# A macaron block on one NeuronCore: second batch's quantisation behind the first batch's parts, one unit's keys on ScalarE's queue, three small operations of each stage on GpSimd

## The chip, the cores and the metric

The kernel runs on one core of a Trainium2 chip. The metric is device microseconds of one execution. A NeuronCore has a matrix engine (TensorE, PE in the rows; its weight loads are PEld), VectorE (DVE), ScalarE (ACT), GpSimd (POOL) and SyncE (SP), each with an instruction stream of its own that runs in order; they wait for one another through semaphores. SP and ScalarE also issue the DMA transfers of this kernel; a DMA instruction on an engine's queue waits its turn behind what stands ahead of it on that engine.

## What is computed

The input is `x`, 8 batches of 512 rows of 128 features. The reference applies three residual steps to it:

```python
def reference(x, ...):
    x = x + 0.5 * ffn(layernorm(x), weight, bias, delta_w, delta_act)      # "f1"
    x = x + attention(layernorm(x), wq, bq, wk, bk, wv, bv)                # "pj" and what follows
    x = x + 0.5 * ffn(layernorm(x), weight, bias, delta_w, delta_act)      # "f2"
    return x

def attention(x, ...):            # 16 heads of 8 features
    xq, xk, xv = (x @ w.T + b).reshape(bs, seq_len, H, HD) for q, k, v
    xq, xk = rope(xq), rope(xk)
    scores = einsum('bhqd,bhkd->bhqk', q, k) / sqrt(HD)
    return einsum('bhqk,bhkd->bhqd', softmax(scores), v)

def ffn(x, ...):                  # blockwise fake quantisation to 4 bits, then a product
    x_q = mxfp4_pseudo_quant(x, delta_act)         # blocks of 32 features
    w_q = mxfp4_pseudo_quant(weight, delta_w)
    return einsum('bsd,od->bso', x_q, w_q) + bias

def mxfp4_pseudo_quant(x, delta):
    amax = max(abs(block)); e = floor(log2(max(amax, TINY)))
    scale = where(amax > 0, exp2(e - 2), 1) * exp2(0.5 * tanh(4 * delta))
    xs = block / scale
    q = sign(xs) * fp4_round(clip(abs(xs), 0, 6))
    return scale * q
```

## The kernel before, in words

All of `x` lies in SBUF (`xres`), a batch as 4 tiles of 128 rows. The kernel runs `slot(b)` for b from -2 to 8, and each slot has 32 steps. Every engine has its own copy of this loop. In step s of slot b the attention of batch b handles one (head, key half) pair: two transposed score products into `st` (`scoresT`), two exponentials on ScalarE (`exp`, `probs`), and every other step the product with the values (`times_v`, into `ot`). Fifteen steps ahead of that, TensorE computes the same scores untransposed into `sc` (`scores`), VectorE takes their row maxima (`maxima`, `negmax`, two per step, 16 per unit of four heads), GpSimd splits a unit's 16 maxima into three bf16 parts (`split_max`), TensorE turns them (`turn_max`), and they are loaded as extra rows of the query features. TensorE takes its instructions in the order written: a transposition that waits holds up the scores behind it.

Queries and keys are kept as three bf16 parts whose sum is the f32 value. After the projection (`project`, `copy_qk`) they get their rope (`rotate`: a product, a product with the pairs swapped by DMA (`swap_pairs`), a sum; for q and then for k), and the parts: `high` (ScalarE), `rest` (f32 less high), `mid` (ScalarE), `low`. Six DMAs on SP write them to DRAM (`write_parts`); when all six have landed (`parts_out`), `load_features` on SP reads them back in the layout of the score products, 24 rows of 2048 bf16 per DMA, three for q and three for k of each unit of four heads. Of the first batch, ScalarE's queue loads the keys of the first two units (`load_keys`). Scores of a unit wait for all six of its loads.

Each of the three norm stages of a batch (`f1`, `pj`, `f2`) runs as `stats` and `aggregate` on VectorE (`mv`), then two 128x4 operations: `ve` (variance plus epsilon) and `nm` (minus the mean); then `rstd` and `nb` on GpSimd (a power, 1 us, and a product) and the normalisation `xn`. A feed-forward stage goes on with the block scales (`block_scales`, rows 0 to 4 of the tile `amax`: largest value, exponent, scale, inverse, and inverse times a factor `invf`), the scaled product (`scale`, `xs`), three operations on VectorE (`exponents`: `xc`, `p`, `magic`), and three more (`quant`: `xs`, `p`, `xq`), then TensorE turns `xq`, ScalarE copies it (`copy_xqT`), TensorE multiplies (`mul_w`) and VectorE adds (`add_ffn`). The rows write `p` for the tile `p2` and `_f` for `_f1` and `_f2`.

Tables of steps set the order (`FFN1`, `PROJ`, `FFN2`): an operation with step t is issued in step t mod 32, in the slot that t div 32 says. `FIRST` overrides them for some stages of the first batches. Batch 0's projection, batch 0's and 1's first feed-forward and the last batch's second are `hurried`: VectorE does more of their work, and without spreading it between maxima. Two lines of the tables matter here:

```python
FIRST["f1", 1] = dict(stats=-16, rstd=-15, norm=-10, amax=-8, scale=-7, expo=-3, quant=-2, turn=8, mul=9)
FIRST["pj", 1] = dict(PROJ, stats=11, rstd=12, norm=14)
```

`("f1", 1)` is the first feed-forward of the second batch. Its `scale` and `quant` run on GpSimd (`hurried_rows` is false for it), its `exponents` on VectorE.

Of the kernel before, what the change touches and what calls it, by code (L numbers as in the profile page):

```python
# [78 lines left out]
FIRST["f1", 1] = dict(stats=-16, rstd=-15, norm=-10, amax=-8, scale=-7, expo=-3, quant=-2, turn=8, mul=9)  # L79
FIRST["pj", 1] = dict(PROJ, stats=11, rstd=12, norm=14)  # L80
# [4 lines left out]
def macaron_kernel(nc, x, wq, bq, wk, bk, wv, bv, w, bias, delta_w, delta_act, ident_in, rope_in, out):  # L85
# [5 lines left out]
    with ExitStack() as ctx:  # L91
# [142 lines left out]
        def hurried_rows(n, b):  # L234

            return hurried(n, b) and (n, b) != ("f1", 1)

# [60 lines left out]
        def _(sp):  # L298
# [38 lines left out]
            def load_features(b, par, half):  # L337
# [8 lines left out]
                for g in (2 * half, 2 * half + 1):  # L346
# [31 lines left out]
        def _(pool):  # L378
# [40 lines left out]
            def rstd(n, b):  # L419

                k, s = bufs[n], LN[n]
                pool.wait_ge(s["stats"], 3 * b + 3)
                if after(b):
                    pool.wait_ge(s["norm"], b)
                nc.gpsimd.tensor_tensor(k["rstd"][:, :], k["ve"][:, :], nhalf[:, :], ALU.pow).then_inc(s["rstd"], 1)  # L425
                pool.wait_ge(s["rstd"], 2 * b + 1)
# [82 lines left out]
            def slot(b, par):  # L509
                for s in range(STEPS):  # L510
# [32 lines left out]
        def _(act):  # L543
# [29 lines left out]
            def norm(n, b, half):  # L573

                k, s = bufs[n], LN[n]
                if half == 0:
                    act.wait_ge(s["rstd"], 2 * b + 2)
# [65 lines left out]
            def load_keys():  # L643
# [3 lines left out]
                for g in range(2):  # L647
                    heads = slice(UH * g, UH * (g + 1))
                    k = scratch_k[0, :, :, heads, :].rearrange("d a h s -> (d a) (h s)")
                    for c in range(PARTS):  # L650
                        act.dma_start(feat["k"][0][PARTS * HD * c:PARTS * HD * (c + 1), heads, :]
                                      .rearrange("r h s -> r (h s)"), k).then_inc(feat_loaded[g], 16)
# [18 lines left out]
            def slot(b, par):  # L671
                for s in range(STEPS):
# [14 lines left out]
                    if b == -2 and s == FIRST["f1", 0]["rstd"]:  # L687
# [31 lines left out]
        def _(dve):  # L719
# [52 lines left out]
            def stats(n, b):  # L772
# [8 lines left out]
                if after(2 * b):  # L781
                    dve.wait_ge(s["rstd"], 2 * b)
# [4 lines left out]
            def aggregate(n, b):  # L787

                k, s = bufs[n], LN[n]
                dve.wait_ge(s["stats"], 3 * b + 1)  # L790
# [152 lines left out]
            def slot(b, par):  # L943
                for s in range(STEPS):
# [23 lines left out]
                    for n, first in (("f2", -1), ("f1", 2)):  # L968
                        for nb, _ in turns(b, par, s, n, "amax", first):
                            block_scales(n, nb, 0)  # L970
                            if hurried(n, nb):
                                for step in range(1, 5):
                                    block_scales(n, nb, step)
                        for later in (1, 2):
                            for nb, _ in turns(b, par, s, n, "amax", first, later=later):
                                if not hurried(n, nb):
                                    block_scales(n, nb, 2 * later)
# [237 lines left out]
```

## Time and profile before

| | us |
|---|---|
| median of 3 runs | 534.62 |
| lowest, highest | 534.57, 535.41 |
| the profiled execution | 534.99 |
| its span, first to last instruction | 533.2 |

| engine | busy us | share of the span |
|---|---|---|
| TensorE | 455.7 | 85% |
| VectorE | 437.7 | 82% |
| ScalarE | 383.2 | 72% |
| GpSimd | 234.0 | 44% |

Times in the rows below are microseconds from the start of the span. In a timeline row the first number is the start, the second the time from the start to the end of the group, then engine, line, operation, output and inputs, shapes and count; in brackets stands how long the engine had been idle before it and what ended that. An engine's share of busy time is an average over a start in which little overlaps (up to some 53 us), a steady part and an end with one batch alone.

### The profile page before, as it was taken

The numbers are of one execution on the slowest core, as the hardware profiler recorded it, in microseconds if no ns is written. First come the engines' busy times: TensorE is split into PE (matmuls) and PEld (weight loads), VectorE is DVE, ScalarE is ACT, GpSimd is POOL, SyncE is SP. The second block draws the span as 40 slices with busy tenths as digits, with TensorE's granted clock in tenths as the row PEclk, the third lists the DMA queues.
The fourth block names the chain that finished last, engine by engine and source line by source line (L and its number), as shares of the span: only waits on it lengthen the run. The fifth ranks groups of instructions, "written<-read, shape, count | busy, mean of one in ns | idle before, by whom it ended". The sixth has DMA issues, their size and how long they took to land.

```text
span 533.2 us, 8358 instructions
## 1 busy us (share of the span) xinstructions
PE 455.7 (85%) x2564; PEld 153.0 (29%) x2564; DVE 437.7 (82%) x996; ACT 383.2 (72%) x750; POOL 234.0 (44%) x340
## 2 busy tenths in 40 slices
PE   2252999999989998999999998999899989998941
PEld 1121232333223232333233323323232323222211
DVE  6863999898899889997999799988997889897125
ACT  7854158678778887787868887787787877777730
POOL 8330065336644465545553656356543624112200
PEclk9985599999999999999999999999999999999995
DMA  5015311321122213221222112221222132100000
GB/s 163 23 49 139 89 52 51 90 92 50 51 90 91 68 36 94 73 75 33 78 77 87 59 51 90 91 71 50 91 85 67 30 91 91 50 2 2 22 0 20
DMA packets 27960, 34.86 MB, mean 65 GB/s; under 512 B 6278, under 2 KB 21260, under 8 KB 27916
## 3 DMA queue, kind: packets, MB, share of 16 engines
q1 hardware_dynamic: 26068, 33.35, 20.6%
q10 hardware_dynamic: 1848, 0.98, 0.7%
q8 instruction: 20, 0.33, 0.3%
q14 instruction: 24, 0.20, 0.1%
HBM read 21.34 MB, written 8.39 MB: 56 GB/s over the span
## 4 chain that ended last, share of the span: by engine, by line
PE 57%; DVE 24%; issue 7%; ACT 5%; POOL 4%; DMA 2%; SPq 0%; POOLq 0%; ACTq 0%; DVEq 0%
PE ot L1138 17%; PE sc L1125 16%; DVE negmax L915 13%; PE st L1114 12%; ACT probs L668 3%; PE misc L1063 2%; PE misc L1080 2%; PE misc L1103 2%; DVE stats_f L784 1%; PE misc L1088 1%; PE misc L1096 1%; PE misc L1058 1%; DMA feat_q<-parts_q 1%; PE misc L1071 1%; PE misc L1047 1%
## 5 line engine op out<-in xcount | busy, mean ns | idle before, releaser
L915 DVE TENSOR_REDUCE negmax<-sc 128x1 f32<-128x512 f32 x512 | 329.6, 682 | 49.2 <-PE sc L1125 48.9
L668 ACT ACTIVATE probs<-st 128x512 f32<-128x512 f32 x512 | 272.7, 599 | 76.9 <-PE st L1114 74.8
L1125 PE MATMUL sc<-feat_k,feat_q 96*128 96x512 bf16 x512 | 186.7, 393 | 18.2 <-DVE negmax L915 10.3
L1114 PE MATMUL st<-feat_q,feat_k 99*128 99x512 bf16 x512 | 155.9, 380 | 8.0 <-ACT probs L668 7.8
L1138 PE MATMUL ot<-probs,vfeat 128*32 128x512 f32 x1024 | 136.2, 604 | 1.1 <-ACT probs L668 1.0
L1125 PEld LDWEIGHTS sc<-feat_k,feat_q 96*128 96x128 bf16 x512 | 49.7, 97 | 169.0 <-DVE negmax L915 101.7
L1114 PEld LDWEIGHTS st<-feat_q,feat_k 99*128 99x128 bf16 x512 | 49.4, 98 | 78.0 <-ACT probs L668 48.9
L466 POOL TENSOR_SCALAR maxparts<-negmax 128x16 bf16<-128x16 f32 x32 | 8.5, 266 | 73.4 <-DVE negmax L915 73.4
L450 POOL TENSOR_TENSOR xs_f<-xc_f,magic_f 128x512 f32<-128x512 f32 x14 | 17.8, 1270 | 36.9 <-DVE magic_f L878 36.9
L425 POOL TENSOR_TENSOR rstd_f<-ve_f,nhalf 128x4 f32<-128x4 f32 x16 | 16.6, 1035 | 37.0 <-DVE nm_f L796 31.7
L1138 PEld LDWEIGHTS ot<-probs,vfeat 128*32 128x32 f32 x1024 | 20.2, 108 | 37.5 <-ACT probs L668 20.0
L443 POOL TENSOR_TENSOR xs_f<-xn_f,amax_f 128x512 f32<-128x512 f32 x14 | 14.7, 1047 | 31.2 <-DVE amax_f L821 31.2
L1047 PE MATMUL misc<-identb,xq_f 128*128 128x128 bf16 x64 | 6.8, 234 | 21.4 <-DVE xq_f L859 17.4
L583 ACT ACTIVATE xn_f<-xres,nb_f,rstd_f 128x128 f32<-128x128 f32 x56 | 24.4, 490 | 0.9 <-POOL nb_f L427 0.9
L506 POOL TENSOR_TENSOR xres<-xres,onorm 128x256 f32<-128x256 f32 x15 | 10.9, 726 | 27.5 <-DVE onorm L931 27.5
L592 ACT COPY xqT_f<-misc 128x512 bf16<-128x512 bf16 x16 | 9.6, 600 | 18.2 <-PE misc L1047 18.2
L485 POOL TENSOR_TENSOR qkswap<-qkswap,ropeT 128x512 f32<-128x512 f32 x14 | 17.8, 1273 | 10.4 <-DMA qkswap<-qkpre 10.4
L425 POOL TENSOR_TENSOR rstd_pj<-ve_pj,nhalf 128x4 f32<-128x4 f32 x8 | 8.3, 1034 | 31.9 <-DVE nm_pj L796 31.9
L883 DVE TENSOR_TENSOR xres<-xres,misc 128x512 f32<-128x512 f32 x16 | 10.9, 683 | 11.8 <-PE misc L1063 11.3
L922 DVE RECIPROCAL recip<-misc 128x32 f32<-128x32 f32 x16 | 5.6, 349 | 16.6 <-PE misc L1103 16.6
L547 ACT COPY feat_k<-zeroone 32x4096 f32<-32x4096 f32 (+1 forms) x4 | 14.4, 3599 | 6.3 <-issue 6.3
L452 POOL TENSOR_TENSOR p_f<-xs_f,magic_f 128x512 f32<-128x512 f32 x14 | 18.1, 1293 | 1.1
(134 smaller groups left out, 461.3 us busy)
## 6 DMA issues: line engine op xcount, KB each, us to landing
feat_q<-parts_q SPq DMA_DIRECT2D x96, 96.0 KB
feat_k<-parts_k SPq DMA_DIRECT2D x90, 96.0 KB
qkswap<-qkpre SPq DMA_DIRECT2D x32, 128.0 KB, 2.0
parts_q<-qkparts_q SPq DMA_DIRECT2D x24, 128.0 KB, 2.3
parts_k<-qkparts_k SPq DMA_DIRECT2D x24, 128.0 KB, 2.3
xres<-in_L_attn_x_dram SPq DMA_DIRECT2D x8, 256.0 KB, 4.9
out_dram<-xres SPq DMA_DIRECT2D x8, 256.0 KB, 2.5
feat_k<-parts_k ACTq DMA_DIRECT2D x6, 96.0 KB
```

What stands on the lines that cost most here:

```text
L425: nc.gpsimd.tensor_tensor(k["rstd"][:, :], k["ve"][:, :], nhalf[:, :], ALU.pow).then_inc(s["rstd"], 1)
L443: nc.gpsimd.tensor_tensor(blocks(k["xs"][:, :]), blocks(k["xn"][:, :]), per_block(k["amax"][:, 4, :]), ALU.mult).then_inc(s["scaled"], 1)
L450: nc.gpsimd.tensor_tensor(k["xs"][:, :], k["xc"][:, :], k["magic"][:, :], ALU.add).then_inc(s["quant"], 1)
L452: nc.gpsimd.tensor_tensor(k["p2"][:, :], k["xs"][:, :], k["magic"][:, :], ALU.subtract).then_inc(s["quant"], 1)
L485: nc.gpsimd.tensor_tensor(qkswap[:, i, :], qkswap[:, i, :], ropeT[:, 1, :], ALU.mult).then_inc(rope_step, 1)
L547: nc.scalar.copy(feat[n][i][low:low + count, :, :].rearrange("r h s -> r (h s)").bitcast(F32), zeroone[low:low + count, value:value + 1].b ...
L583: ins = nc.scalar.activation(k["xn"][:, t * D:(t + 1) * D], xb(b, t * D, D), ACT.Identity, bias=k["nb"][:, t:t + 1], scale=k["rstd"][:, t: ...
L668: nc.scalar.activation(probs[:, s % US, j * S:(j + 1) * S], st[:, bank(2 * s + j), :], ACT.Exp, scale=SCALE).then_inc(exp_done, 1)
L915: nc.vector.tensor_reduce(negmax[:, g, j:j + 1], sc[:, bank(16 * g + j), :], AX.X, ALU.max, negate=True).then_inc(sc_maxed, 1)
L1114: nc.tensor.matmul(st[:, bank(2 * s + j), :], feat["k"][par][0:MROWS, h, kb * P:(kb + 1) * P], feat["q"][par][0:MROWS, h, :], start=True, ...
L1125: nc.tensor.matmul(sc[:, bank(16 * g + j), :], feat["q"][par][0:SROWS, h, t * P:(t + 1) * P], feat["k"][par][0:SROWS, h, :], start=True, s ...
L1138: ins = nc.tensor.matmul(ot[VW * i:VW * (i + 1), :], vfeat[par][:, kb, UH * g + i, :], probs[:, UH * (kb // 2) + i, S * (kb % 2):S * (kb % ...
```

## The change

Four edits.

1. The second batch's first feed-forward: `expo` and `quant` move from steps -3 and -2 to step 9 (of slot -1), `turn` and `mul` two steps later, and its `quant` runs on VectorE. `scale` stays on GpSimd. The statistics of its projection move two steps later.
2. ScalarE's `load_keys` loads the keys of the first unit only, and stands ahead of the second batch's `copy_xqT`. SP loads the second unit's keys, between that unit's queries.
3. `ve` and `nm` of every norm stage run on GpSimd, in front of `rstd`.
4. The last row of the block scales (inverse times `invf`) runs in front of `scale`, on `scale`'s engine: GpSimd for all stages but the first batch's first and the last batch's second feed-forward.

```diff
-FIRST["f1", 1] = dict(stats=-16, rstd=-15, norm=-10, amax=-8, scale=-7, expo=-3, quant=-2, turn=8, mul=9)
-FIRST["pj", 1] = dict(PROJ, stats=11, rstd=12, norm=14)
+FIRST["f1", 1] = dict(stats=-16, rstd=-15, norm=-10, amax=-8, scale=-7, expo=9, quant=9, turn=10, mul=11)
+FIRST["pj", 1] = dict(PROJ, stats=13, rstd=14, norm=16)
...
@@ SP, load_features
-                        if (b, half) != (0, 0):
+                        if (b, g) != (0, 0):
...
@@ GpSimd, rstd
-                pool.wait_ge(s["stats"], 3 * b + 3)
+                pool.wait_ge(s["stats"], 2 * b + 2)
                 if after(b):
                     pool.wait_ge(s["norm"], b)
+                nc.gpsimd.tensor_scalar(k["ve"][:, :], k["mv"][:, :, 1], EPS, None, ALU.add).then_inc(s["rstd"], 1)
+                nc.gpsimd.tensor_scalar(k["nm"][:, :], k["mv"][:, :, 0], -1.0, None, ALU.mult).then_inc(s["rstd"], 1)
+                pool.wait_ge(s["rstd"], 4 * b + 2)
                 nc.gpsimd.tensor_tensor(k["rstd"][:, :], k["ve"][:, :], nhalf[:, :], ALU.pow).then_inc(s["rstd"], 1)
...
@@ GpSimd, scale (the same two lines on VectorE)
+                pool.wait_ge(s["scale"], 5 * b + 4)
+                nc.gpsimd.tensor_scalar(k["amax"][:, 4, :], k["amax"][:, 2, :], invf[:, 0:1], None, ALU.mult).then_inc(s["scale"], 1)
...
@@ GpSimd, slot
-                            if not hurried_rows(n, nb):
+                            if not hurried(n, nb) or (n, nb) == ("f1", 1):
                                 scale(n, nb)
                         for nb, _ in turns(b, par, s, n, "quant", first):
-                            if not hurried_rows(n, nb):
+                            if not hurried(n, nb):
                                 quant(n, nb)
...
@@ ScalarE, load_keys and slot
-                for g in range(2):
-                    heads = slice(UH * g, UH * (g + 1))
+                heads = slice(0, UH)
...
+                    if b == -1 and s == FIRST["f1", 1]["turn"]:
+                        load_keys()
                     if b == -1 and s == PROJ["load"][0] % STEPS:
-                        load_keys()
                         feature_rows("k", 1, 1)
...
@@ VectorE, aggregate
-                dve.wait_ge(s["stats"], 3 * b + 2)
-                nc.vector.tensor_scalar(k["ve"][:, :], k["mv"][:, :, 1], EPS, None, ALU.add)
-                nc.vector.tensor_scalar(k["nm"][:, :], k["mv"][:, :, 0], -1.0, None, ALU.mult).then_inc(s["stats"], 1)
```

The order of the instructions shows three places. On VectorE in the start, from the first rope product of batch 0 (`qkT`, `qkswap`) to its `low` (`qkparts` from `qkrest`), before:

```order
L890 TENSOR_TENSOR qkT_q<-qkpre,ropeT 128x512
L870 TENSOR_SCALAR xc_f<-xs_f 128x512
L874 TENSOR_SCALAR p_f<-xc_f 128x512
L878 TENSOR_SCALAR magic_f<-p_f 128x512
L893 TENSOR_TENSOR qkswap<-qkswap,ropeT 128x512
L895 TENSOR_TENSOR qkT_q<-qkT_q,qkswap 128x512
L890 TENSOR_TENSOR qkT_k<-qkpre,ropeT 128x512
L893 TENSOR_TENSOR qkswap<-qkswap,ropeT 128x512
L895 TENSOR_TENSOR qkT_k<-qkT_k,qkswap 128x512
L901 TENSOR_TENSOR qkrest_q<-qkT_q,qkparts_q 128x512
```

and the end of the same stretch now, from the last two operations of the parts to the first maxima:

```order
L898 TENSOR_TENSOR qkrest_k<-qkT_k,qkparts_k 128x512
L904 TENSOR_TENSOR qkparts_k<-qkrest_k,qkparts_k 128x512
L867 TENSOR_SCALAR xc_f<-xs_f 128x512
L871 TENSOR_SCALAR p_f<-xc_f 128x512
L875 TENSOR_SCALAR magic_f<-p_f 128x512
L850 TENSOR_TENSOR xs_f<-xc_f,magic_f 128x512
L852 TENSOR_TENSOR p_f<-xs_f,magic_f 128x512
L856 TENSOR_TENSOR xq_f<-p_f,amax_f 128x512
L880 TENSOR_TENSOR xres<-xres,misc 128x512
L785 BN_STATS stats_pj<-xres 128x6 x4
L793 BN_AGGR mv_pj<-stats_pj 128x2 x4
L912 TENSOR_REDUCE negmax<-sc 128x1 x37
```

The three `exponents` left the place behind the first rope product and stand, with the three operations of `quant` that were GpSimd's, behind the last `low`, ahead of the add, the statistics and the first maxima. On ScalarE, at the same time, from the last part to the fill of feature rows, before:

```order
L627 CAST qkparts_k<-qkrest_k 128x512
L592 COPY xqT_f<-misc 128x512
L651 DMA feat_k<-parts_k 24x2048 x6
L547 COPY feat_k<-zeroone 3x4096
L583 ACTIVATE xn_pj<-xres,nb_pj,rstd_pj 128x128 x4
```

and now:

```order
L628 CAST qkparts_k<-qkrest_k 128x512
L651 DMA feat_k<-parts_k 24x2048 x3
L593 COPY xqT_f<-misc 128x512
L548 COPY feat_k<-zeroone 3x4096
L584 ACTIVATE xn_pj<-xres,nb_pj,rstd_pj 128x128 x4
```

The key loads went from six to three and in front of the copy of the second batch's `xq`. On GpSimd in a steady batch, from the split of a unit's maxima (`maxparts`, `maxrest`) to the quantisation of the first feed-forward, now:

```order
L467 TENSOR_SCALAR maxparts<-negmax 128x16
L469 TENSOR_TENSOR maxrest<-negmax,maxparts 128x16
L471 TENSOR_SCALAR maxparts<-maxrest 128x16
L473 TENSOR_TENSOR maxparts<-maxrest,maxparts 128x16
L421 TENSOR_SCALAR ve_f<-mv_f 128x4
L422 TENSOR_SCALAR nm_f<-mv_f 128x4
L424 TENSOR_TENSOR rstd_f<-ve_f,nhalf 128x4
L426 TENSOR_TENSOR nb_f<-nm_f,rstd_f 128x4
L438 TENSOR_SCALAR amax_f<-amax_f,invf 128x16
L444 TENSOR_TENSOR xs_f<-xn_f,amax_f 128x512
```

Before, `ve`, `nm` and the `amax` row stood on VectorE, between maxima; the other seven rows stood here in this order.

## Rows read from the trace of the kernel before

**Rows 1.** Busy time by stretch: TensorE, weight loads, VectorE, ScalarE, GpSimd, clock, DMA.

```profile
46.00:52.60 6.60, 0.00 (x0) 0.00 (x1) 1.19 (x9) 3.50 (x1) 1.22 (x2) 0.50 0.61 158
...
60.00:67.50 7.50, 7.42 (x17) 2.80 (x18) 6.59 (x11) 0.84 (x2) 0.94 (x4) 0.50 0.02 4
...
193.20:250.09 56.89, 54.20 (x321) 18.30 (x320) 51.36 (x119) 45.12 (x93) 30.37 (x42) 1.00 0.23 71
```

**Rows 2.** Chain that ended last, in order of time (start, length), around the loads.

```profile
43.56 2.30 DMA parts_k<-qkparts_k
...
47.58 4.98 DMA feat_q<-parts_q
```

**Rows 3.** Timeline of VectorE in the start (start, length).

```profile
33.45 1.20 DVE L893 TENSOR_TENSOR qkswap<-qkswap,ropeT 128x512 f32<-128x512 f32 x1 [0.69 <-DMA qkswap<-qkpre]
...
37.70 0.68 DVE L893 TENSOR_TENSOR qkswap<-qkswap,ropeT 128x512 f32<-128x512 f32 x1
...
39.02 0.68 DVE L901 TENSOR_TENSOR qkrest_q<-qkT_q,qkparts_q 128x512 f32<-128x512 f32 x1
...
42.37 0.69 DVE L907 TENSOR_TENSOR qkparts_k<-qkrest_k,qkparts_k 128x512 bf16<-128x512 f32 x1 [0.68 <-ACT qkparts_k L627]
44.98 0.69 DVE L883 TENSOR_TENSOR xres<-xres,misc 128x512 f32<-128x512 f32 x1 [1.92 <-PE misc L1063]
...
46.60 0.38 DVE L792 BATCH_NORM_AGGREGATE mv_pj<-stats_pj 128x2 f32<-128x6 f32 x4
...
53.24 10.86 DVE L915 TENSOR_REDUCE negmax<-sc 128x1 f32<-128x512 f32 x18 [5.99 <-PE sc L1125]
```

**Rows 4.** Timelines of GpSimd and ScalarE in the start.

```profile
35.85 1.38 POOL L456 TENSOR_TENSOR xq_f<-p_f,amax_f 128x512 bf16<-128x512 f32 x1
...
32.51 3.60 ACT L547 COPY feat_k<-zeroone 32x4096 f32<-32x4096 f32 x1
36.35 0.62 ACT L623 CAST qkparts_q<-qkT_q 128x512 bf16<-128x512 f32 x1 [0.25 <-DVE qkT_q L895]
...
45.93 3.12 ACTq L651 DMA_DIRECT2D feat_k<-parts_k  x6
```

**Rows 5.** Timeline of VectorE at the end: quantisation to residual add.

```profile
522.80 0.43 DVE L870 TENSOR_SCALAR xc_f<-xs_f 128x512 f32<-128x512 f32 x1
...
529.77 0.69 DVE L883 TENSOR_TENSOR xres<-xres,misc 128x512 f32<-128x512 f32 x1 [3.44 <-PE misc L1063]
```

**Rows 6.** Timelines of VectorE, TensorE and GpSimd in a steady batch.

```profile
198.59 0.37 DVE L792 BATCH_NORM_AGGREGATE mv_f<-stats_f 128x2 f32<-128x6 f32 x4
...
199.19 3.07 DVE L915 TENSOR_REDUCE negmax<-sc 128x1 f32<-128x512 f32 x5
...
204.66 0.42 DVE L870 TENSOR_SCALAR xc_f<-xs_f 128x512 f32<-128x512 f32 x1
...
199.93 0.39 PE L1125 MATMUL sc<-feat_k,feat_q 96*128 96x512 bf16 x1 [0.47 <-DVE negmax L915]
...
199.96 0.25 POOL L466 TENSOR_SCALAR maxparts<-negmax 128x16 bf16<-128x16 f32 x1 [0.78 <-DVE negmax L915]
...
202.38 1.05 POOL L443 TENSOR_TENSOR xs_f<-xn_f,amax_f 128x512 f32<-128x512 f32 x1
```

**Rows 7.** Groups of small operations by shape: count, busy us, mean ns.

```profile
L466 POOL TENSOR_SCALAR maxparts<-negmax 128x16 bf16<-128x16 f32 x32 | 8.5, 266 | 73.4 <-DVE negmax L915 73.4
...
L427 POOL TENSOR_TENSOR nb_pj<-nm_pj,rstd_pj 128x4 f32<-128x4 f32 x8 | 1.6, 201 | 0.6
...
L412 POOL TENSOR_SCALAR biasr<-biasp,ident 3x256 f32<-3x256 bf16 x1 | 0.9, 912 | 0.1
...
L821 DVE TENSOR_SCALAR amax_f<-amax_f,invf 128x16 f32<-128x16 f32 x16 | 3.7, 234 | 0.1
```

**Rows 8.** Timelines of VectorE and GpSimd in the last norm stage.

```profile
517.15 0.38 DVE L792 BATCH_NORM_AGGREGATE mv_f<-stats_f 128x2 f32<-128x6 f32 x4
...
517.88 1.04 POOL L425 TENSOR_TENSOR rstd_f<-ve_f,nhalf 128x4 f32<-128x4 f32 x1 [20.15 <-DVE nm_f L796]
```

More of the change, by code:

```diff
@@ L232, in hurried @@
             return (n, b) in (("f1", 0), ("pj", 0), ("f1", 1), ("f2", B - 1))
-        def hurried_rows(n, b):
-            return hurried(n, b) and (n, b) != ("f1", 1)
         def qk_bank(b, j):
@@ L421, in rstd @@
                 k, s = bufs[n], LN[n]
-                pool.wait_ge(s["stats"], 3 * b + 3)
+                pool.wait_ge(s["stats"], 2 * b + 2)
                 if after(b):
                     pool.wait_ge(s["norm"], b)
+                nc.gpsimd.tensor_scalar(k["ve"][:, :], k["mv"][:, :, 1], EPS, None, ALU.add).then_inc(s["rstd"], 1)
+                nc.gpsimd.tensor_scalar(k["nm"][:, :], k["mv"][:, :, 0], -1.0, None, ALU.mult).then_inc(s["rstd"], 1)
+                pool.wait_ge(s["rstd"], 4 * b + 2)
                 nc.gpsimd.tensor_tensor(k["rstd"][:, :], k["ve"][:, :], nhalf[:, :], ALU.pow).then_inc(s["rstd"], 1)
-                pool.wait_ge(s["rstd"], 2 * b + 1)
+                pool.wait_ge(s["rstd"], 4 * b + 3)
                 nc.gpsimd.tensor_tensor(k["nb"][:, :], k["nm"][:, :], k["rstd"][:, :], ALU.mult).then_inc(s["rstd"], 1)
@@ L576, in norm @@
                 if half == 0:
-                    act.wait_ge(s["rstd"], 2 * b + 2)
+                    act.wait_ge(s["rstd"], 4 * b + 4)
                     if n == "pj" and after(b):
@@ L646, in load_keys @@
                 act.wait_ge(parts_out, 96)
-                for g in range(2):
-                    heads = slice(UH * g, UH * (g + 1))
[L649 to L652, printed above, removed]
+                heads = slice(0, UH)
+                k = scratch_k[0, :, :, heads, :].rearrange("d a h s -> (d a) (h s)")
+                for c in range(PARTS):
+                    act.dma_start(feat["k"][0][PARTS * HD * c:PARTS * HD * (c + 1), heads, :]
+                                  .rearrange("r h s -> r (h s)"), k).then_inc(feat_loaded[0], 16)
             def copy_out(b, g):
@@ L780, in stats @@
                     dve.wait_ge(x_attended, 2 * b + 2)
-                if after(2 * b):
-                    dve.wait_ge(s["rstd"], 2 * b)
+                if after(b):
+                    dve.wait_ge(s["rstd"], 4 * b)
                 for t in range(T):
@@ L789, in aggregate @@
                 k, s = bufs[n], LN[n]
-                dve.wait_ge(s["stats"], 3 * b + 1)
+                dve.wait_ge(s["stats"], 2 * b + 1)
                 for t in range(T):
@@ L815, in block_scales @@
                     nc.vector.tensor_scalar(m[:, 3, :], m[:, 1, :], TINY_FLOOR, 0.25, ALU.max, ALU.mult).then_inc(s["scale"], 1)
-                elif step == 3:
+                else:
                     dve.wait_ge(s["scale"], a + 3)
                     nc.vector.reciprocal(m[:, 2, :], m[:, 3, :]).then_inc(s["scale"], 1)
-                else:
-                    dve.wait_ge(s["scale"], a + 4)
-                    nc.vector.tensor_scalar(m[:, 4, :], m[:, 2, :], invf[:, 0:1], None, ALU.mult).then_inc(s["scale"], 1)
             def blocks(ap):
@@ L831, in norm @@
                 k, s = bufs[n], LN[n]
-                dve.wait_ge(s["rstd"], 2 * b + 2)
+                dve.wait_ge(s["rstd"], 4 * b + 4)
                 if n != "pj" and b > 0:
@@ L842, in scale @@
                 k, s = bufs[n], FF[n]
+                dve.wait_ge(s["scale"], 5 * b + 4)
+                nc.vector.tensor_scalar(k["amax"][:, 4, :], k["amax"][:, 2, :], invf[:, 0:1], None, ALU.mult).then_inc(s["scale"], 1)
                 dve.wait_ge(s["scale"], 5 * b + 5)
@@ L971, in slot @@
                             if hurried(n, nb):
-                                for step in range(1, 5):
+                                for step in range(1, 4):
                                     block_scales(n, nb, step)
[L974 to L977, printed above, removed]
+                        for nb, _ in turns(b, par, s, n, "amax", first, later=1):
+                            if not hurried(n, nb):
+                                block_scales(n, nb, 2)
                         for nb, _ in turns(b, par, s, n, "scale", first):
-                            if hurried_rows(n, nb):
+                            if hurried(n, nb) and (n, nb) != ("f1", 1):
                                 scale(n, nb)
```

2 lines of the change are left out of this document (1 added, 1 removed).

## The prediction, made before the changed kernel had run

> **What bounds the kernel now.** I first read busy time by stretch, then the chain that ended last, then the instructions of each engine in order. In the steady part one batch takes 56.89 us, with TensorE busy 54.20 and VectorE 51.36 of it [rows 1]: TensorE has some 2.7 us of gaps in a batch, and only VectorE work that causes such a gap is worth anything. Before the steady part TensorE does nothing at all between 46.0 and 52.6 us [rows 1]. So there are two stages to cost: the start (up to the first row maximum at 53.24 us [rows 3]) and the repeated batch; then the end, where the last batch runs alone.
>
> In the start the chain runs through the first batch's rope and parts. The last of six stores of the parts is issued at 43.56 and lands 2.30 us later; the loads go out, the last query load of the first unit is issued at 47.58 and lands 4.98 us later [rows 2]; then scores begin. The reader is to see in the VectorE rows that the same kind of instruction, a two-input 128x512 operation, takes 1.20 us at 33.45 but 0.68 at 37.70 [rows 3], and in the GpSimd rows that the second batch's quantisation (three such operations in a row, the last from 35.85) runs until 37.23, just before the fast one [rows 4].
>
> **The start, step by step.** *Quantisation moved behind the parts.* The three `exponents` operations stood before the rope's swap product, which waited 0.69 us longer for its DMA anyway [rows 3]: taking them out gains nothing there. What gains is that GpSimd is silent during the rope. From the swap product at 33.45 to the first `rest` at 39.02 are five operations in 5.57 us. At the undisturbed spacing of the pair 37.70 to 39.02 (two in 1.32; I take 0.71 each, since the second hand-over is shortened) they need 3.55. One loss stands ahead of it: `rstd` of the first projection norm now has the two small operations on GpSimd, +0.25 (costed under the tail). So `rest` starts at 33.45 + 0.25 + 3.55 = 37.25 instead of 39.02: **-1.77**. It needs the high part from ScalarE, which has a 3.60 us fill from 32.51 in front of it [rows 4]: fill end 36.36 with the +0.25, copy 0.62 [rows 4], so 37.0, just in time. Behind it the chain of parts and stores is unchanged, so the stores land at 45.86 - 1.77 = 44.1.
>
> *Loads.* Now ScalarE issues six key loads, 3.12 us from 45.93 [rows 4], beside SP's query loads. From 46.0 to 52.6 the DMA engines move 158 GB/s [rows 1], 1.04 MB, or 10.6 loads of 24 rows of 2048 bf16 (98 KB; the shape stands with the change), while the first unit needs six: the second unit's keys on ScalarE's queue went ahead of the first unit's queries. With three of them moved to SP, behind the first unit's queries, some two to three loads fewer stand ahead: 2.5 x 6.6/10.6 = 1.5 us. Bounds: nothing, and the four and a half loads that are too many, 2.8. I take 1.4, near the middle: scores could begin 3.2 us earlier and the first maximum stand at 50.1; with nothing, at 51.5.
> The Trainium skill, DMA: Bandwidth & Descriptors, section SWDGE vs HWDGE vs iDMA, says that a DMA engine takes its queues in turn. By that rule SP's three query loads had to let only three key loads pass, and removing the fourth to sixth would change nothing, so the first maximum would stand at 51.5 and the sum come to rival 1's; the 10.6 loads moved by the landing speak against it here.
>
> *What is late next.* VectorE. The second batch's quantisation now lies between the parts and the first maximum: the last `low` ends at 43.06 - 1.77 = 41.3 (it ran from 42.37 for 0.69 [rows 3]). The same sequence, alone, stands at the end of the program: from `xc` at 522.80 to the end of the residual add, 529.77 + 0.69, 7.66 us, TensorE's transposes and products included [rows 5]. ScalarE's copy in it now stands behind the key loads, which wait for the stores: 44.1 + three issues of 0.52 = 45.7, against 45.55 when the copy could start, +0.2. The add ends at 49.15; statistics and aggregation follow it as now, from the add's end at 45.67 to 46.98 [rows 3], 1.3 us. So VectorE is free at 50.45, later than the 50.1 of the loads, and the first maximum starts there: 53.24 - 50.45 = **-2.8**. If the loads gain nothing: -1.8. The second unit's keys, now between the queries on SP, are 12 loads in at 0.62 each from 45, some 53, and wanted 16 maxima of 0.60 after 50.4 [rows 3], at 60; that costs nothing.
>
> **The repeated batch.** *`ve` and `nm` off VectorE.* Only one of the three norm stages of a batch has TensorE waiting on VectorE, the one of the second feed-forward. There the aggregation ends at 198.96 and the next maximum starts at 199.19 [rows 6]; without the two it follows the aggregation at once, which is 0.23 less, or up to 0.08 more where neighbouring operations overlap, as the next operation here starts before the one ahead is shown as ended; I take 0.29. TensorE's next score sat idle 0.47 for a maximum there [rows 6], so the shift is passed on. In the other norm stages of the batches, twelve, VectorE waits for TensorE soon after and I cost them at nothing; uncovered, they would be worth the same again. Seven stages on the path: 7 x 0.29 = **-2.0**. Bounds: 0, if the next wait takes it up, and -5.5 with the other twelve.
>
> *`amax` times the inverse off VectorE:* it is the last small operation of its stage, behind which VectorE waits for TensorE again, so nothing; uncovered, fourteen times 0.23 [rows 7], 3.3. What GpSimd does next waited for it before too.
>
> *On GpSimd* the three operations lengthen the queue: the split of the maxima starts at 199.96, the scaled block product `xs` runs from 202.38 to 203.43, and VectorE wants that at 204.66 [rows 6]: 1.23 us in hand. Prices: a 128x16 scalar operation took 0.27, a 128x4 one 0.20; the pointer-scalar form on 3x256 took 0.91 [rows 7]. These have 4 to 16 elements per partition, so I go by the first two: 0.27 + 0.22 + 0.30 with gaps, about 0.85. 0.4 us remain in hand, so nothing is late. The split stands ahead of them in the queue and is not delayed.
>
> **The tail.** In the last feed-forward the aggregation ends at 517.53 and `rstd` starts at 517.88 [rows 8]. These 0.35 us hold VectorE's two operations and the hand-over. On GpSimd the two take 0.27 + 0.22 = 0.49; if VectorE's share of the 0.35 is between 0.1 and 0.35, the loss is 0.14 to 0.39: I take **+0.25** (by the 0.91 price, 1.5). The multiplication stays on VectorE there.
>
> **Sum.** -2.8 - 2.0 + 0.25 = -4.55. The profiled execution took 534.99 (span 533.2), 0.37 above the median of the runs; on the median of 534.62 I forecast **530.0**.
>
> **Rivals.**
> 1. *The start gains only what the rope gains* (loads not helped, or ScalarE held longer before the copy that the second batch's product, and behind it all scores, wait for): -1.8 instead of -2.8, 531.1. For it: two paths end within 0.4 us of each other. 18%.
> 2. *The steady relief is taken up* by TensorE's other gaps or by ScalarE: -2.55 in all, 532.1. For it: TensorE is at 95%. Against: its gap at this place is released by the maximum. 15%.
> 3. *VectorE's relief is worth more*: the stages costed at nothing, and the first batch, give another 1 to 2 us: 528.5. 15%.
> 4. *The clock returns earlier.* From 60.0 to 67.5 TensorE is busy 7.42 of 7.50 us at a granted 0.50, 1.2 GHz [rows 1]. If the shorter idle stretch brings 2.4 GHz sooner, at most half of the dense part from 62 on, some 2 us: 527.8. Against: the idle stretch keeps some 8 us. 6%.
> 5. *Slower.* GpSimd's three operations outlast the 1.23 us in hand, VectorE's `xc` waits and with it every maximum queued behind, in seven batches. Net zero is reached where the three take 1.88 together (7 x (1.88 - 1.52) = 2.55). At the pointer price of 0.91 each they take 2.73: +8.5 in the batches, -2.8 at the start, +1.5 in the tail, 541.8. 5%.
> 6. *No net change* (rival 1 with rival 2 and a longer tail), 534: 5%.
>
> The forecast itself has 36%. A measurement of this kernel tells changes of over 0.2%, 1.07 us. Faster 0.89, same 0.06, slower 0.05. The range takes in rivals 1 to 3 and part of 4: 527.4 to 532.6; the forecast's own is 529 to 531.
>
> **What would show it.** The rope's operations on VectorE at 0.69 with GpSimd idle; `rest` near 37.3; the first score near 49.5 and the first maximum near 50.4 right behind the aggregation; a batch period near 56.6; no wait of `xc` for `xs`; `rstd` in the last stage 0.25 later behind its aggregation. Wrong would make it: GpSimd's small operations at over 0.6 us, key loads that still land at 50.8, or a period that stays at 56.89.

## The result, and the profile after

| | before | changed |
|---|---|---|
| median, us | 534.77 | 528.59 |
| lowest, highest | 534.57, 535.41 | 528.04, 529.05 |
| span of the profiled execution | 533.2 | 527.2 |
| busy: TensorE, VectorE, GpSimd | 455.7, 437.7, 234.0 | 454.2, 429.1, 245.8 |

The ratio is 0.9886 (95% interval 0.9874 to 0.9898): 6.2 us or 1.1% faster, where 4.55 were forecast. Both medians are of four runs. A second series gave 528.51 against 534.72, ratio 0.9890 (0.9875 to 0.9905).

**The start.** VectorE, then ScalarE and TensorE, in the timeline of the changed kernel; the rows answer to [rows 3] and [rows 4].

```profile
33.26 0.69 DVE L890 TENSOR_TENSOR qkswap<-qkswap,ropeT 128x512 f32<-128x512 f32 x1 [1.95 <-DMA qkswap<-qkpre]
...
35.20 0.68 DVE L890 TENSOR_TENSOR qkswap<-qkswap,ropeT 128x512 f32<-128x512 f32 x1
...
36.52 0.68 DVE L898 TENSOR_TENSOR qkrest_q<-qkT_q,qkparts_q 128x512 f32<-128x512 f32 x1
...
39.87 0.69 DVE L904 TENSOR_TENSOR qkparts_k<-qkrest_k,qkparts_k 128x512 bf16<-128x512 f32 x1 [0.68 <-ACT qkparts_k L628]
40.48 0.42 DVE L867 TENSOR_SCALAR xc_f<-xs_f 128x512 f32<-128x512 f32 x1
...
47.87 0.69 DVE L880 TENSOR_TENSOR xres<-xres,misc 128x512 f32<-128x512 f32 x1 [3.87 <-PE misc L1059]
...
49.49 0.38 DVE L793 BATCH_NORM_AGGREGATE mv_pj<-stats_pj 128x2 f32<-128x6 f32 x4
50.04 2.48 DVE L912 TENSOR_REDUCE negmax<-sc 128x1 f32<-128x512 f32 x4 [0.17 <-PE sc L1121]
...
35.58 0.62 ACT L624 CAST qkparts_q<-qkT_q 128x512 bf16<-128x512 f32 x1
...
43.44 1.58 ACTq L651 DMA_DIRECT2D feat_k<-parts_k  x3
45.12 0.59 ACT L593 COPY xqT_f<-misc 128x512 bf16<-128x512 bf16 x1 [5.29 <-PE misc L1043]
...
49.39 1.03 PE L1121 MATMUL sc<-feat_k,feat_q 96*128 96x512 bf16 x2 [1.57 <-DMA feat_q<-parts_q]
```

Before, TensorE's first score stood here:

```profile
52.60 2.00 PE L1125 MATMUL sc<-feat_k,feat_q 96*128 96x512 bf16 x4 [7.66 <-DMA feat_q<-parts_q]
```

Both swap products now take 0.69 and 0.68. `rest` starts at 36.52 in place of 39.02 and the loads go out at 43.44 in place of 45.93: 2.50 us earlier. From the loads' issue to the first score are 5.95 us in place of 6.67, another 0.72. The first maximum moves from 53.24 to 50.04, by 3.20. VectorE is ready for it at 49.87 and then waits 0.17 for TensorE's score, so the loads and VectorE end almost together.

**The steady batch.** Timelines of VectorE and GpSimd, which answer to [rows 6].

```profile
194.83 0.37 DVE L793 BATCH_NORM_AGGREGATE mv_f<-stats_f 128x2 f32<-128x6 f32 x4
...
195.12 3.05 DVE L912 TENSOR_REDUCE negmax<-sc 128x1 f32<-128x512 f32 x5
195.86 0.25 POOL L467 TENSOR_SCALAR maxparts<-negmax 128x16 bf16<-128x16 f32 x1 [0.43 <-DVE negmax L912]
...
197.14 0.23 POOL L421 TENSOR_SCALAR ve_f<-mv_f 128x4 f32<-128x4 f32 x1
...
199.06 0.34 POOL L438 TENSOR_SCALAR amax_f<-amax_f,invf 128x16 f32<-128x16 f32 x1
...
199.48 1.05 POOL L444 TENSOR_TENSOR xs_f<-xn_f,amax_f 128x512 f32<-128x512 f32 x1
...
200.56 0.43 DVE L867 TENSOR_SCALAR xc_f<-xs_f 128x512 f32<-128x512 f32 x1
```

The next maximum starts 0.29 after the aggregation's start, 0.60 before. GpSimd's split of the maxima (`maxparts`), which waits for them, comes earlier with it: 1.03 after the aggregation's start, 1.37 before. From the split's start, `xs` ends at 4.67 in place of 3.47, so the three small operations lengthen GpSimd's row by 1.20 us. VectorE's `xc` starts 4.70 behind the split in both kernels. Of the 1.23 us in hand 0.03 are left; `xc` does not wait in a steady batch, but nothing is left in hand.

**Tail, and busy time by stretch** (columns as in [rows 1]). The tail's rows answer to [rows 8].

```profile
510.83 0.38 DVE L793 BATCH_NORM_AGGREGATE mv_f<-stats_f 128x2 f32<-128x6 f32 x4
511.30 0.23 POOL L421 TENSOR_SCALAR ve_f<-mv_f 128x4 f32<-128x4 f32 x1 [19.88 <-DVE mv_f L793]
...
511.92 1.04 POOL L424 TENSOR_TENSOR rstd_f<-ve_f,nhalf 128x4 f32<-128x4 f32 x1
```

```profile
60.00:67.50 7.50, 6.81 (x18) 2.55 (x17) 6.04 (x11) 1.53 (x3) 2.01 (x5) 0.68 0.11 39
138.28:194.83 56.55, 54.19 (x320) 18.30 (x319) 50.79 (x112) 45.09 (x94) 32.48 (x51) 1.00 0.23 71
```

From the aggregation's start to `rstd` are 1.09 us, 0.73 before: +0.36. A batch takes 56.55 in place of 56.89; TensorE's busy time in it is the same, and its gaps are shorter. Read by the attention's output rows, the shift against before is 3.20 at the first maximum, 3.43 after the first batch, grows by 0.35 in each of six batches to 5.50, by 0.82 in the last to 6.32, and the tail gives 0.36 back: 5.96, the 6.0 by which the spans differ.

### The profile page after: what moved, and what is told of

The parts are those of the page before. It is cut to its first block, busy times and chain, and to the rows that moved or that the text cites. A ratio compares the mean times of both kernels' runs of the same rounds, so it can differ in the third digit from the quotient of the medians.

```text
span 527.2 us, 8358 instructions
## 1 busy us (share of the span) xinstructions
PE 454.2 (86%) x2564; PEld 152.3 (29%) x2564; DVE 429.1 (81%) x937; ACT 383.4 (73%) x750; POOL 245.8 (47%) x399
## 4 chain that ended last, share of the span: by engine, by line
PE 58%; DVE 22%; issue 7%; POOL 5%; ACT 5%; DMA 2%; SPq 0%; POOLq 0%; ACTq 0%; DVEq 0%
PE ot L1134 18%; PE sc L1121 16%; PE st L1110 12%; DVE negmax L912 12%; ACT probs L668 3%; PE misc L1059 2%; PE misc L1076 2%; PE misc L1099 2%; DVE stats_f L785 1%; PE misc L1084 1%; PE misc L1092 1%; PE misc L1054 1%; PE misc L1067 1%; PE misc L1043 1%; DVE amax_f L805 1%
## 5 line engine op out<-in xcount | busy, mean ns | idle before, releaser
L1110 PEld LDWEIGHTS st<-feat_q,feat_k 99*128 99x128 bf16 x512 | 49.4, 98 | 78.6 <-ACT probs L668 50.2
L451 POOL TENSOR_TENSOR xs_f<-xc_f,magic_f 128x512 f32<-128x512 f32 x13 | 16.5, 1273 | 29.0 <-DVE magic_f L875 29.0
L421 POOL TENSOR_SCALAR ve_pj<-mv_pj 128x4 f32<-128x4 f32 x8 | 1.8, 228 | 40.6 <-DVE mv_pj L793 40.6
L421 POOL TENSOR_SCALAR ve_f<-mv_f 128x4 f32<-128x4 f32 x16 | 3.7, 229 | 34.5 <-DVE mv_f L793 29.8
L453 POOL TENSOR_TENSOR p_f<-xs_f,magic_f 128x512 f32<-128x512 f32 x13 | 16.5, 1272 | 1.0
L785 DVE BATCH_NORM_STATS2 stats_f<-xres 128x6 f32<-128x128 f32 x64 | 13.8, 278 | 2.7 <-DMA xres<-in_L_attn_x_dram 2.6
```

The costliest lines, as they stand in the source:

```text
L451: nc.gpsimd.tensor_tensor(k["xs"][:, :], k["xc"][:, :], k["magic"][:, :], ALU.add).then_inc(s["quant"], 1)
L453: nc.gpsimd.tensor_tensor(k["p2"][:, :], k["xs"][:, :], k["magic"][:, :], ALU.subtract).then_inc(s["quant"], 1)
L785: ins = nc.vector.bn_stats(k["stats"][:, t, :], xb(b, t * D, D))
L1110: nc.tensor.matmul(st[:, bank(2 * s + j), :], feat["k"][par][0:MROWS, h, kb * P:(kb + 1) * P], feat["q"][par][0:MROWS, h, :], start=True, ...
```

## The experiments

Times are medians of 4 to 12 runs. A difference in brackets is taken from the median of before in the same series: 534.63 for experiments 1 to 3, 534.55 for 4 to 7, 534.72 for 8. 528.51 is the changed kernel's median of experiment 8; what is set against it comes from another series, so some 0.2 us of such a difference can be the series.

**1. The start alone, and the small operations alone.** Two kernels that share the change between them. `e1_start_only` is the kernel before with edits 1 and 2, `e2_small_only` the one with edits 3 and 4:

```diff
 e1: FIRST["f1", 1], FIRST["pj", 1], load_keys, load_features and quant's engine as changed
 e2: aggregate, rstd, block_scales and scale as changed
```

> The kernel before with the first two parts of the change alone: exponents and quantisation of f1 1 behind the four parts of pj 0 and on VectorE, ScalarE's queue with three key loads. ve, nm and the fourth row of amax stay on VectorE. Theory (two independent parts): the start gives about 3.0 us (first maximum at about 50.2), each batch takes 56.9 as before, the tail does not change, so the time is about 531.8. Rival (the start gets its gain from the small operations): about 534 to 534.5, and the first maximum stays near 53.

> The kernel before with the third part alone: ve, nm and the fourth row of amax on GpSimd. Theory: the start gains 0.2 us, the batches 0.35 each (2.1 to 2.5 over six to seven of them), the last batch's f2 stage about 0.8, and the tail loses 0.36, so about 531.5 to 532, with e1 the two differences add up to that of the whole change, 6.2 us, to within 0.5. Rival (the relief of a batch comes from a TensorE that is granted its clock earlier because of the earlier start): about 534.6, batches of 56.9.

Measured: 531.39 (-3.24) and 532.61 (-2.02). Batches take 56.90 in the first (4 batches, 137.71 to 365.31 by the aggregations) and 56.55 in the second (141.59 to 367.79): the relief of a batch is the small operations', the gain of the start the reordering's, and neither rival stands. The second time lies 0.6 above what was expected. The two do not add up to 6.2 to within 0.5; they fall 0.9 short. The intervals of the two ratios (0.9924 to 0.9951, 0.9941 to 0.9973) are together wider than that. In the rows, e2's first maximum is at 53.61, 0.37 later than before: its loads took 7.21 us to the first score against 6.67.

**2. The order undone.** `e3_no_reorder` is the changed kernel without edit 1; ScalarE still has three key loads, at the old place.

```diff
-FIRST["f1", 1] = dict(..., expo=9, quant=9, turn=10, mul=11)
+FIRST["f1", 1] = dict(..., expo=-3, quant=-2, turn=8, mul=9)      # and quant on GpSimd
```

> The changed kernel with its first part undone: exponents of f1 1 ahead of the parts of pj 0 and the quantisation on GpSimd again; ScalarE's queue still has three key loads, at their old place, and the small operations stay on GpSimd. Theory: the whole of the rope's 2.5 us comes from the order, and the loads get 0.2 to 0.7 for having one half less on one queue, so the time is 1.8 to 2.5 above the changed kernel, about 530.5 to 531.1. Rival (three key loads in place of six on ScalarE's queue are what the start gains): at most 0.5 above the changed kernel, about 529.

Measured: 530.87, 2.36 above the changed kernel's 528.51. The rope is back to its old pace (`rest` at 38.85), and what edit 1 gives, with the place of `load_keys` ahead of the copy, is 2.1 (first maxima) to 2.4 (medians).

It gives a second comparison: e3 differs from e2 only in the key loads. First the rows of e2, then of e3: ScalarE's loads, TensorE's first score.

```profile
45.75 3.11 ACTq L652 DMA_DIRECT2D feat_k<-parts_k  x6
...
52.96 1.46 PE L1121 MATMUL sc<-feat_k,feat_q 96*128 96x512 bf16 x3 [8.21 <-DMA feat_q<-parts_q]
```

```profile
45.78 1.57 ACTq L651 DMA_DIRECT2D feat_k<-parts_k  x3
...
51.53 2.00 PE L1120 MATMUL sc<-feat_k,feat_q 96*128 96x512 bf16 x4 [6.76 <-DMA feat_q<-parts_q]
```

7.21 us from issue to score with six, 5.75 with three. Here, where VectorE is free early, the whole difference reaches the first maximum: 53.61 to 52.17.

**3. The loads undone.** `e4_six_key_loads` is the changed kernel without edit 2's count.

```diff
-                heads = slice(0, UH)
+                for g in range(2):
+                    heads = slice(UH * g, UH * (g + 1))
```

> The changed kernel with the second part undone: six key loads on ScalarE's queue, none of the first batch's first half on SP's, still ahead of the copy of the quantised rows of f1 1. Theory: the copy starts 4.7 us later than it does with three issues of 1.58 us, so f1 1's sums come behind the first maximum, and the loads land 0.7 later: 0.7 to 2.0 above the changed kernel, about 529.3 to 530.6. Rival (the engines take their queues in turn and the number on a queue does not matter; the copy has time in hand): 0 to 0.2, about 528.7, with the first maximum at 50.0.

Measured: 529.78, 1.27 above 528.51. The copy of `xq` starts at 46.74 in place of 45.12, VectorE is free at 51.41, and the first maximum starts there, 1.37 later. The loads take 7.16, 1.2 more than in the first profile of the changed kernel, where 0.7 was expected. Theory right, on both of its paths: the loads alone would have moved the first maximum by almost as much. (The copy's delay is 1.6, three issues more, not the 4.7 that the expectation named by a slip.)

**4. GpSimd beside the rope.** `e5_gpsimd_beside_rope` adds three additions on GpSimd whose result nobody uses.

```diff
+                pool.wait_ge(qk_swapped[0], 32)
+                for i in range(3):
+                    nc.gpsimd.tensor_tensor(bufs["f2"]["p2"][:, :], xb(2), xb(2), ALU.add).then_inc(spare, 1)
+                    pool.wait_ge(spare, i + 1)
```

> The changed kernel with work added whose result nobody uses: three additions of 128x512 on GpSimd, begun when q's swapped halves have landed, so that they run beside the five operations of the rope on VectorE. Theory (the rope gained 0.74 us more than forecast because GpSimd's quantisation no longer shares the memory port with VectorE's operations of two inputs): the five operations go from 0.69 us to 0.9 to 1.2 each, the stores and loads behind them come 1 to 2.5 later, and so does the end: 529.6 to 531.1. Rival (only the exponents taken out of VectorE's queue matter): operations stay at 0.69, time within 0.2 of the changed kernel.

Measured: 530.95, 2.4 above 528.51. Timeline of VectorE and GpSimd:

```profile
33.37 4.37 POOL L466 TENSOR_TENSOR p_f<-xres 128x512 f32<-128x512 f32 x3 [4.56 <-DMA qkswap<-qkpre]
33.99 1.41 DVE L903 TENSOR_TENSOR qkT_q<-qkT_q,qkswap 128x512 f32<-128x512 f32 x1
35.33 1.52 DVE L898 TENSOR_TENSOR qkT_k<-qkpre,ropeT 128x512 f32<-128x512 f32 x1
...
36.77 1.52 DVE L901 TENSOR_TENSOR qkswap<-qkswap,ropeT 128x512 f32<-128x512 f32 x1
...
38.94 0.68 DVE L909 TENSOR_TENSOR qkrest_q<-qkT_q,qkparts_q 128x512 f32<-128x512 f32 x1
```

With the exponents still out of VectorE's queue, three operations on GpSimd give back the whole gain: `rest` at 38.94, as before the change. Three of VectorE's operations take 1.41 to 1.52 in place of 0.69, each about as long as one of GpSimd's (4.37 / 3 = 1.46). The rival is dead: what edit 1 gives is GpSimd's silence. The Trainium skill, SBUF — State Buffer, section Who interferes with whom, says that a VectorE instruction with two inputs in SBUF contends with a GpSimd instruction that reads SBUF, and that the lock on the ports they share is exclusive; the 1.46 and 1.52 agree.

**5. Two stages back on VectorE.** `e6_first_last_vectore` has `ve` and `nm` on VectorE for the first projection norm and the last feed-forward norm, and on GpSimd elsewhere.

```diff
+            return (n, b) in (("pj", 0), ("f2", B - 1))      # alone(n, b): ve and nm on VectorE
```

> The changed kernel with ve and nm on VectorE again in two stages only, pj 0 and f2 of the last batch, where GpSimd's three operations stand in a row that all else waits for. Theory: rstd of pj 0 starts 0.3 to 0.4 earlier and the rope with it, and the tail gains 0.36: 0.6 to 0.8 below the changed kernel, about 527.9. Rival (the start is bound by the swap's landing and not by rstd): only the tail's 0.36, about 528.2.

Measured: 528.13 (527.96 to 528.54), ratio to before 0.9881 (0.9869 to 0.9894). The swap product starts at 32.76 in place of 33.26, the first maximum at 49.40 in place of 50.04, and from the last aggregation to `rstd` are 0.82 in place of 1.09. The rows show both gains. The median is the lowest of the study, 6.4 below before in its own series where the changed kernel is 6.2 below, but that is less than such a measurement can tell from no change.

**6. The `amax` row.** `e7_amax_vectore` has it on VectorE again.

```diff
-                nc.gpsimd.tensor_scalar(k["amax"][:, 4, :], k["amax"][:, 2, :], invf[:, 0:1], None, ALU.mult)
+                    nc.vector.tensor_scalar(m[:, 4, :], m[:, 2, :], invf[:, 0:1], None, ALU.mult)
```

> The changed kernel with the fourth row of amax on VectorE again, ve and nm stay on GpSimd. Theory: the row is off the chain of a steady batch, so its move gives 0 per batch; in the last batch it gives the 0.5 us that the last stage gained beyond the steady relief: 0 to 0.5 above the changed kernel, 528.6 to 529.1. Rival (a third of the relief of 0.35 per batch is the row's): 0.12 x 7 = 0.8 above, about 529.4, with batches of 56.67.

Measured: 529.45, 0.9 above 528.51. The time is the rival's, the rows are not: batches take 56.55 (138.21 to 364.43, four). All of it comes at the end, 0.26 in the batch before the last and 0.53 in the last. The rows of the last batch's last unit, first e7, then the changed kernel:

```profile
483.97 0.22 DVE L817 TENSOR_SCALAR amax_f<-amax_f,invf 128x16 f32<-128x16 f32 x1
...
485.29 0.54 POOL L465 TENSOR_SCALAR maxparts<-negmax 128x16 bf16<-128x16 f32 x1
...
487.17 0.24 PE L1092 MATMUL misc<-identb,maxparts 128*48 128x128 bf16 x1 [0.97 <-POOL maxparts L471]
```

```profile
483.41 0.34 POOL L438 TENSOR_SCALAR amax_f<-amax_f,invf 128x16 f32<-128x16 f32 x1 [7.63 <-DVE amax_f L816]
...
484.84 0.25 POOL L467 TENSOR_SCALAR maxparts<-negmax 128x16 bf16<-128x16 f32 x1
...
486.42 0.24 PE L1092 MATMUL misc<-identb,maxparts 128*48 128x128 bf16 x1 [0.44 <-POOL maxparts L473]
```

On VectorE the row stands between the last maxima, and GpSimd's split of these maxima, behind `xs` in its row, starts later. Of the 0.53, 0.13 is the last maximum and 0.11 the way from it to the split. The other 0.30 is the split itself, which takes 1.88 us to TensorE's turn in e7 and before, and 1.58 in the changed kernel. But e1, with the `amax` row on VectorE, has 1.58 too, and its last batch is 0.29 shorter than before's: this part is not shown to be the row's, and why the split's operations take longer in two kernels stays open. In the batch before the last the parts do not add up: e7 loses 0.26 there, the kernel with `ve` and `nm` undone (e9) 0.37, and before, without either edit, 0.35.

**7. What GpSimd has in hand.** `e8_gpsimd_slack` adds a power, whose result nobody uses, behind `nb` of every second feed-forward but the last.

```diff
+                    nc.gpsimd.tensor_tensor(idle[:, :], k["ve"][:, :], nhalf[:, :], ALU.pow).then_inc(spare, 1)
```

> The changed kernel with work added whose result nobody uses: one more power of 1.04 us on GpSimd behind nb in the f2 stage of every batch but the last. Theory (GpSimd had 1.23 us in hand before xc, and the small operations used 0.85 of it): xs comes about 0.65 later than xc can, and every batch takes 0.65 longer: about 4.5 us above the changed kernel, 533.1. Rival (xs was never near the chain, since the maximum that it needs comes later than GpSimd's three operations): 0 to 0.3, about 528.7.

Measured: 535.33, 6.8 above 528.51 and 0.3% slower than before (ratio 1.003, 1.0017 to 1.0043). Timelines of VectorE and GpSimd:

```profile
201.48 1.05 POOL L450 TENSOR_TENSOR xs_f<-xn_f,amax_f 128x512 f32<-128x512 f32 x1
...
202.56 0.43 DVE L873 TENSOR_SCALAR xc_f<-xs_f 128x512 f32<-128x512 f32 x1 [0.88 <-POOL xs_f L450]
```

A batch takes 57.51, 0.96 more than 56.55, for an operation of 1.01: nothing was in hand, where the theory had 0.4. Seven of the twelve runs took 534.9 to 535.4 us and five 537.3 to 537.5; the profile is one of the first group, and what the others lost is not known. In one batch of the profile (310.88 to 369.85, 58.97 us) the granted clock also fell to half, from about 324.5 to 327.9, which no other kernel here showed: 1.5 us more.

**8. `ve` and `nm` on VectorE everywhere, and the changed kernel again.** `e9_stats_vectore` undoes edit 3 alone; `a1_changed_again` is the changed kernel.

```diff
+            return True      # alone(n, b)
```

> The changed kernel with ve and nm on VectorE again in every stage; only the fourth row of amax stays on GpSimd. Theory (the relief of a batch is that ve and nm no longer stand in front of a maximum on VectorE, 0.35 per batch; the amax row gives only the 0.5 of the last stage): batches of 56.9, start 0.5 earlier as in the kernel with two stages changed back, tail 0.36 earlier, less 0.3 in the last f2 stage: 7 x 0.35 + 0.3 - 0.86 = 1.9 above the changed kernel, about 530.5. Rival (the relief is GpSimd's later xs, that is the order of GpSimd's operations and not VectorE's row): batches stay at 56.55, and the time is 0.5 below the changed kernel, about 528.1.

> The changed kernel itself, beside e9 on one chip, to hold the sum of e1 and e2 against it. Both theories: 528.0 to 529.1. If the first scores start 0.3 us sooner or later than 49.39 here, with the same issue of the loads, the loading time spreads from run to run, and the 0.72 us that the loads seemed to give in the first profile is one draw of it; a fixed price would give 49.3 to 49.5.

Measured: 531.63 (-3.1) and 528.51 (-6.2). Batches of e9 take 56.88 (138.55 to 366.06, four): all but 0.02 of the relief of 0.35 is VectorE's row, and not GpSimd's. The kernel is 3.1 above the changed one, where 1.9 was expected. Of the 3.0 by which the spans differ, 0.65 is the final store: the span ends 3.37 us behind the last addition, against 2.72; and the start did not gain 0.5, it lost 0.3. The reason stands in the set-up of the first microseconds, VectorE and GpSimd, first e9, then the changed kernel:

```profile
7.11 0.53 POOL L406 TENSOR_SCALAR biasin<-biasin 3x128 f32<-3x128 f32 x1
...
8.21 0.78 DVE L759 TENSOR_TENSOR wtmp<-wtmp 128x128 f32<-128x128 f32 x1
...
10.91 0.69 DVE L814 TENSOR_REDUCE amax_f<-xn_f 128x16 f32<-128x512 f32 x1
```

```profile
7.71 0.55 POOL L402 TENSOR_SCALAR biasin<-biasin 3x128 f32<-3x128 f32 x1
...
7.90 0.29 DVE L754 TENSOR_TENSOR wtmp<-wtmp 128x128 f32<-128x128 f32 x1
...
9.83 0.69 DVE L805 TENSOR_REDUCE amax_f<-xn_f 128x16 f32<-128x512 f32 x1
```

With `ve` and `nm` of the first norm ahead of it, GpSimd's preparation of the bias starts 0.6 later, and VectorE's weight preparation passes it: VectorE is 1.08 us ahead at `amax`. That the bias work is what slows the weight preparation (0.78 against 0.29 for one product) is read from these rows alone. Part of it is given back to the same bias work, and 0.7 is left at the first projection's statistics (21.32 against 22.02). Moving the bias work out of the way altogether was not tried.

In a1 the first score comes at 49.21, 5.69 us after the loads' issue, against 49.39 and 5.95 in the first profile: between the two cases expected. Over all twelve profiles, three key loads took 5.05 to 5.95 (nine kernels, mean 5.68), six 6.67 to 7.21 (three, mean 7.01): 1.33 apart, with single profiles up to 0.63 from their mean.

## Why the prediction was right, and where its terms were off

The forecast was 530.0, measured 528.59: inside the range of 527.4 to 532.6 but below the forecast's own 529 to 531. Sign and mechanism were right and the gain too small, by 1.4 us of the span's 5.96. Term by term, in the profiled execution:

| step of the prediction | forecast | measured |
|---|---|---|
| `rest` starts | 37.25 (-1.77) | 36.52 (-2.50) |
| loads, with three keys less on ScalarE | -1.4 | -0.72 (this pair), -1.33 (means), -1.44 (e2 to e3) |
| VectorE free, first maximum | 50.45, -2.8 | 49.87, 50.04, -3.20 |
| first batch | 0 | -0.23, not traced |
| second feed-forward norm, seven stages | 7 x -0.29 = -2.0 | 6 x -0.35 - 0.28 = -2.4 |
| `amax` row | 0 | 0 in a steady batch, -0.53 in the last, 0.3 of it not shown to be the row's |
| three small operations on GpSimd | 0.85 of 1.23 in hand | 1.20 of 1.23 |
| tail | +0.25 | +0.36 |

**Rope: the right mechanism, mis-sized by 0.73.** The five operations took 3.26 and not 3.55: all have the spacing of an undisturbed pair, 0.65, where I took 0.71. The swap product came at 33.26 and not at 33.70: the small operations ahead of `rstd` cost 0.5 there and not 0.25, but GpSimd's later set-up gave 0.7, which the prediction did not look for. Experiment 4 shows that GpSimd's silence is the cause, experiment 5 the 0.5, and experiment 8 the 0.7.

**Loads: right on the mean, and by luck in the profile.** The 1.4 from "10.6 loads moved by the landing" is what e2 and e3 differ by, and near the difference of the means. My reading of the rule weighed against it (the Trainium skill, DMA: Bandwidth & Descriptors, section SWDGE vs HWDGE vs iDMA), that the fourth to sixth key load would change nothing, is not borne out: they cost 1.3 to 1.4. How they cost it, by standing ahead of the queries or by a share of the transfer engines, no run separates. In the profiled pair the loads gave only 0.72. That the path through them ended at 50.04, where 50.1 was forecast, is luck: the rope gave 0.73 more and the loads 0.68 less. "VectorE is late next" was right to within 0.2 us, since VectorE is ready 0.17 sooner; which of the two ends last changes with the loads' spread (VectorE in e1, e4, e7 and e9, the loads in the first profile). Rival 1, the loads not helping, is refuted.

**Batches: right, 0.06 small.** 0.35 is beyond the 0.29 that I took from the rows, 0.23 to 0.31; rival 2, that the relief is taken up, did not happen in any batch.

**GpSimd in hand: right by 0.03, the price too low by 0.35.** "0.4 us remain in hand, so nothing is late" came true only just. The three operations were costed at 0.85 and lengthen GpSimd's row by 1.20, of which 0.75 is `ve` and `nm` and 0.44 the `amax` row (e7 and e9, which take one of the two off GpSimd, keep 0.48 and 0.79 in hand). The 0.85 was added up from durations with small gaps. From start to start an operation takes 0.31 (`ve`, `nm`) and 0.42 (`amax`) in the changed kernel's rows, and there are hand-overs beside. Measured from the aggregation, `xs` comes only 0.86 later, which looks like the 0.85; but that is 1.20 less the 0.34 by which the split starts earlier, and `xc` comes earlier by the same 0.34. The same prices were too low in the tail (+0.36 for +0.25) and ahead of the first projection's `rstd` (0.5 for 0.25). Rival 5's point of no change, three operations of 1.88 together, does not suffer from this; the change came within 0.03 of where each further microsecond costs one, and e8 shows that side, 0.96 a batch.

**The `amax` row: missed.** It is free in a steady batch, where VectorE waits for TensorE behind it, and its move goes with 0.53 in the last batch, where the split of the last maxima stands behind `xs` on GpSimd and nothing covers it. The prediction looked at a steady batch only.

The difference of 1.4 lies in the start (0.4), the first batch (0.2), the batches (0.4) and the last batch (0.5), less 0.1 in the tail. The time came out at rival 3's 528.5, but only the first batch's part is its mechanism.

## What to carry to other kernels

Price a small operation on another engine's queue by the step from its start to the next one's start, hand-over included, and not by its duration: here 1.20 us for three, where durations with small gaps gave 0.85, and 1.23 were in hand. Measure slack from an event that both sides wait for (here the split of the maxima): from the aggregation, which the edit moved against it, the cost looked like 0.86. GpSimd's two-input work beside VectorE's two-input operations doubles them (0.69 to 1.5 here), so when VectorE's row is the chain, GpSimd's silence is worth more than the operations taken out of the row. Look at the first and the last batch apart from the steady one: an operation that is free in steady state can stand on the chain there.

## What was not expected of the hardware

The granted clock returns at different times in two executions of one kernel. Busy time by stretch and TensorE's timeline, first of the changed kernel's first profile, then of a1:

```profile
62.00:64.00 2.00, 2.00 (x4) 0.78 (x3) 1.57 (x3) 0.00 (x0) 0.00 (x0) 0.50 0.06 14
64.00:66.00 2.00, 1.71 (x5) 0.40 (x3) 1.16 (x2) 0.69 (x1) 0.77 (x1) 0.79 0.00 0
...
62.46 1.91 PE L1076 MATMUL misc<-xnT,wqkT 128*128 128x512 f32 x2
```

```profile
62.00:64.00 2.00, 2.00 (x7) 0.84 (x5) 1.59 (x4) 0.43 (x1) 0.00 (x0) 0.82 0.06 14
64.00:66.00 2.00, 1.23 (x5) 0.44 (x5) 2.00 (x4) 0.26 (x1) 1.26 (x1) 1.00 0.17 66
...
62.28 1.26 PE L1076 MATMUL misc<-xnT,wqkT 128*128 128x512 f32 x2
```

In both, TensorE had been busy almost without a gap since 49.4 and 49.2. Its clock went from 0.50 (1.2 GHz) to 1.00 (2.4 GHz) some 2 us earlier in the second. The f32 projection in between, which VectorE's next maxima wait behind, took 1.26 in place of 1.91; the aggregation that follows (74.78 against 75.79) is 1.0 us earlier, while the first maxima were 0.2 apart, and the times are 528.06 and 529.05. In the twelve profiles this stretch, from the first maximum to that aggregation, takes 24.8 to 25.8 us. It is 25.75 in both profiles that the rows above compare, so their 5.96 holds nothing of it. By the two executions of one kernel, about 1 us of a single execution goes with the clock, and rival 4 is neither confirmed nor refuted as a gain of the change.
